# Full attention: scores from two-part float32r stacks with two heads side by side, in another order of issue

## The reference

```python
q = (x @ wq.T).reshape(b, s, NH, HD).transpose(0, 2, 1, 3)
k = (x @ wk_a.T @ wk_b.T).reshape(b, s, NH, HD).transpose(0, 2, 1, 3)
v = (x @ wv_a.T @ wv_b.T).reshape(b, s, NH, HD).transpose(0, 2, 1, 3)
q = _apply_decoupled_rope(q, cosf, sinf, DROPE)
k = _apply_decoupled_rope(k, cosf, sinf, DROPE)
scores = jnp.einsum('bhqd,bhkd->bhqk', q, k) / np.float32(np.sqrt(HD))
attn = jax.nn.softmax(scores, axis=-1)
out = jnp.einsum('bhqk,bhkd->bhqd', attn, v)
out = out.transpose(0, 2, 1, 3).reshape(b, s, NH * HD)
return out @ wo.T
```

## Time and profile before

| | us |
|---|---|
| median of 3 runs | 4984.07 (4980.47 to 4986.2) |
| the profiled execution | 4988.85 |
| its span, first to last instruction | 4987.1 |
| projections and setup, to the first row score | 315 |
| full attention, first column score to last copy of the sums | 364.6 to 1921.7 |

### The profile page before, as it was taken

One profiled execution on the slowest core, in us unless ns is written; L12 is line 12 of the kernel. 1 busy time (PEld: TensorE's weight loads), 2 busy tenths in 40 slices (PEclk: granted clock), 3 DMA queues, 4 the chain that ended last, 5 costly groups with the idle time before them and its releaser, 6 DMA issues. The chain is left out here.

```text
span 4987.1 us, 97545 instructions
## 1 busy us (share of the span) xinstructions
PE 4492.7 (90%) x27802; PEld 2756.6 (55%) x27802; DVE 3736.9 (75%) x8989; ACT 2758.3 (55%) x6177; POOL 1684.7 (34%) x2440
## 2 busy tenths in 40 slices
PE   4779999999999997489999996999799999997998
PEld 2423333332323333367777775888577777776887
DVE  6978888888888884878888885554488887884554
ACT  1317666766666774056666664333466666663333
POOL 3620000000000001445555554433355555554555
PEclk8869999999999998799999997999999999998999
DMA  4762323232323323610000001111100000002221
GB/s 156 244 137 40 56 43 59 40 59 40 59 40 59 46 35 124 205 43 26 25 23 26 24 25 50 43 53 46 48 25 24 26 24 25 23 23 81 78 64 50
DMA packets 385590, 288.63 MB, mean 58 GB/s; under 512 B 64284, under 2 KB 346392, under 8 KB 385056
## 3 DMA queue, kind: packets, MB, share of 16 engines
q1 hardware_dynamic: 385056, 282.19, 23.6%
HBM read 178.74 MB, written 102.83 MB: 56 GB/s over the span
## 5 line engine op out<-in xcount | busy, mean ns | idle before, releaser
L949 DVE TENSOR_REDUCE fa_mx<-fa_pR 128x1 f32<-128x512 f32 x2048 | 1276.3, 684 | 207.8 <-PE fa_pR L826 198.5
L925 ACT ACTIVATE fa_P<-fa_pS 128x512 f32<-128x512 f32 x2048 | 1077.2, 601 | 531.1 <-PE fa_pS L849 528.3
L1557 POOL TENSOR_TENSOR wa_pn<-wa_pr,wa_ri 128x512 f32<-128x512 f32 x512 | 700.6, 1369 | 616.3 <-DVE wa_ri L1613 602.9
L826 PE MATMUL fa_pR<-fa_K,fa_Q 96*128 96x512 bf16 x2048 | 804.1, 393 | 29.3 <-DMA fa_K<-parts_d 28.8
L849 PE MATMUL fa_pS<-fa_Q,fa_K 98*128 98x512 bf16 x2048 | 784.2, 386 | 26.8 <-issue 22.4
L1179 POOL TENSOR_TENSOR ao_xn<-ao_xn,ao_mod 128x1024 f32<-128x1024 f32 x16 | 37.6, 2347 | 1742.3 <-DVE ao_xn L1144 1742.3
L1493 ACT ACTIVATE wa_pr<-wa_sm,wa_mn 128x256 f32<-128x256 f32 x1024 | 510.5, 502 | 178.3 <-DVE wa_mn L1605 176.9
L862 PE MATMUL fa_pO<-fa_P,fa_V 128*32 128x512 f32 x4096 | 552.0, 611 | 5.9 <-ACT fa_OT L914 5.2
L849 PEld LDWEIGHTS fa_pS<-fa_Q,fa_K 98*128 98x128 bf16 x2048 | 199.2, 98 | 638.2 <-ACT fa_P L925 437.5
L1345 PE MATMUL wa_pQK<-wa_wqkv,wa_xT 128*128 128x512 f32 x1536 | 420.6, 410 | 5.8 <-DVE wa_qa L1650 5.8
L2051 ACT ACTIVATE ff_gl<-ff_pG,ff_b 128x512 f32<-128x512 f32 x192 | 132.1, 688 | 475.4 <-PE ff_pG L1992 475.4
(11 more groups left out here) (191 smaller groups left out, 7358.4 us busy)
## 6 DMA issues: line engine op xcount, KB each, us to landing
parts_d<-pj_parts SPq DMA_DIRECT2D x96, 256.0 KB, 2.8
fa_Q<-parts_d SPq DMA_DIRECT2D x192, 128.0 KB, 4.7
fa_K<-parts_d SPq DMA_DIRECT2D x192, 128.0 KB, 7.3
v_d<-pj_v SPq DMA_DIRECT2D x16, 1024.0 KB, 6.0
fa_V<-v_d SPq DMA_DIRECT2D x32, 512.0 KB, 9.9
pj_x<-in_L_attn_x SPq DMA_DIRECT2D x16, 512.0 KB, 6.7
att_d<-fa_att SPq DMA_DIRECT2D x32, 256.0 KB, 3.2
ao_att<-att_d SPq DMA_DIRECT2D x16, 512.0 KB, 4.7
```

The source lines that it names most:

```text
L826: nc.tensor.matmul(row_tile(), Qs[0:SROWS, s, h, q * P:(q + 1) * P], Ks[0:SROWS, s, h, half * 512:(half + 1) * 512], start=True, stop=True ...
L925: nc.scalar.activation(Pr[:, k % 2, h, half * 512:(half + 1) * 512], pS[:, (s * exped.per + u) % T, :], ACT.Exp).then_inc(exped.sem, 1)
L949: nc.vector.tensor_reduce(mx[:, j // 2, j % 2:j % 2 + 1], row_tile(), AX.X, ALU.max).then_inc(row_free, 1)
L1557: nc.gpsimd.tensor_tensor(pn[:, hp % 2], pr[:, hp % 2], inv, ALU.mult).then_inc(s["weighted"].sem, 1)
```

## The change

q and k are split into two float32r parts instead of three bfloat16 ones; ScalarE writes the first, one subtraction on VectorE the second. `second` and `third` are gone. The stacks become float32r with three blocks of 16 rows to a head, and two heads stand in one stack: one at partitions 0 to 47 (maxima and ones at 48 and 49), one at 64 to 111 (112 and 113). Each score matmul has 48 or 50 rows, and those of the two heads follow each other, into different banks. VectorE reduces both heads' row scores at once, from a slot of two banks; there are two such slots (ROW_T).

A group is now taken in two halves of the queries, 8 steps to each. A step has the column scores of heads 0 and 1, both row pairs of the next group, the column scores of heads 2 and 3, and the sums of the step before. Maxima, copies, transposes, divisions and stores go by halves. The negative maximum is transposed in float32 and split after it; it reaches the stack by 16 DMAs to a group. Row scores run one group ahead, no longer two steps more. The first loads wait for the rows of ones. The constant `identb` and its copy in the setup are gone.

```diff
-Q_PARTS = (0, 1, 2, 0, 1, 0)
-K_PARTS = (0, 0, 0, 1, 1, 2)
+Q_PARTS = (0, 0, 1)
+K_PARTS = (0, 1, 0)
...
-        parts_d = dram("parts_d", [2, 3, D, B, N], BF16)
+        parts_d = dram("parts_d", [2, 2, D, B, N])
...
-        parts = sb("pj_parts", [P, 2, 2, 3, KT, CH], BF16)
-        res = sb("pj_res", [P, 2, KT, CH])
+        parts = sb("pj_parts", [P, 2, 2, 2, KT, CH], F32R)
...
-                def rest(n, p, qk):
+                def low(n, p, qk):
                     dve.wait_ge(hi_ready.sem, hi_ready.upto(n, qk + 1))
-                    if again(n):
-                        dve.wait_ge(lows.sem, lows.upto(n - 1, qk + 1))
-                    nc.vector.tensor_tensor(res[:, qk], (pQ, pK)[qk][:], parts[:, p, qk, 0],
-                                            ALU.subtract).then_inc(split.sem, 1)
-                def second(n, p, qk):
-                    dve.wait_ge(split.sem, split.upto(n, 2 * qk + 1))
-                    if later(n) and qk == 0:
-                        dve.wait_ge(stored.sems[p], stored.upto(n - 2))
-                    nc.vector.tensor_copy(parts[:, p, qk, 1], res[:, qk]).then_inc(split.sem, 1)
+                    nc.vector.tensor_tensor(parts[:, p, qk, 1], (pQ, pK)[qk][:], parts[:, p, qk, 0].bitcast(F32),
+                                            ALU.subtract).then_inc(lows.sem, 1)
                 def body(n, r, following=True):
                     if following:
-                        stats_of(n + 2, (r + 2) % R, range(0, 4))
-                    rest(n, r % 2, 0)
+                        stats_of(n + 2, (r + 2) % R, range(0, 6))
+                    low(n, r % 2, 0)
...
-                def third(n, p, qk):
-                    pool.wait_ge(split.sem, split.upto(n, 2 * qk + 2))
-                    nc.gpsimd.tensor_tensor(parts[:, p, qk, 2], res[:, qk], parts[:, p, qk, 1],
-                                            ALU.subtract).then_inc(lows.sem, 1)
...
+        Qs = sb("fa_Q", [P, NB, PAIRS, N], F32R)
+        Ks = sb("fa_K", [P, NB, PAIRS, N], F32R)
...
+        pS = ctx.enter_context(nc.psum_tensor("fa_pS", [P, T, HALF], F32))
+        pR = ctx.enter_context(nc.psum_tensor("fa_pR", [P, ROW_T, 2, HALF], F32))
+        pO = ctx.enter_context(nc.psum_tensor("fa_pO", [P, HALF], F32))
...
+                            src = parts_d[qk, part].rearrange("(g a e d) b t -> e d g a b t", d=HD, e=2, a=PAIRS)
+                            for e in range(2):
+                                at = e * TOP + slot * HD
+                                one = src[e][:, bass.ds(g, 1), :, bass.ds(b, 1), :]
+                                sp.dma_start(stack[at:at + HD, s].bitcast(F32),
+                                             one.rearrange("d g a b t -> d (g a) (b t)")).then_inc(stack_in.sems[s], 16)
...
+                def max_rows(n, s, half):
+                    sp.wait_ge(row_free, max_use(n, half) + 1)
                     for part in range(2):
+                        for e in range(2):
+                            for a in range(PAIRS):
+                                at, col = e * TOP + SROWS + part, (e * PAIRS + a) * QB
+                                dst = Qs[at:at + 1, s, a, half * HALF:(half + 1) * HALF].bitcast(F32)
+                                src = nrow[col:col + QB, s, half, part, :].bitcast(F32)
+                                sp.dma_start(dst, src).then_inc(max_in[half].sems[s], 16)
...
+                sp.wait_ge(ones, NB)
                 load(0, 0)
                 load(1, 1)
+                max_rows(0, 0, 0)
                 def body(n, s):
+                    max_rows(n, s, 1)
+                    if not (isinstance(n, int) and n + 2 >= GROUPS):
+                        load(n + 2, (s + 2) % NB)
                     if not is_first(n):
+                        store(n - 1, 1)
                     if not is_last(n):
+                        max_rows(n + 1, (s + 1) % NB, 0)
+                    store(n, 0)
                 drive(sp, body)
+                store(GROUPS - 1, 1)
...
+                def row_slot():
+                    base, k = use
+                    if not (isinstance(base, int) and base + k < ROW_T):
+                        pe.wait_ge(row_free, base + k - ROW_T + 1)
+                    use[1] += 1
+                    first = base if isinstance(base, int) else 0
+                    return pR[:, (first + k) % ROW_T]
...
+                    q, a, kh = j // (2 * PAIRS), j // 2 % PAIRS, j % 2
...
+                    slot = row_slot()
+                    for e in range(2):
+                        at = e * TOP
+                        last = nc.tensor.matmul(slot[:, e, :], Qs[at:at + SROWS, s, a, q * P:(q + 1) * P],
+                                                Ks[at:at + SROWS, s, a, kh * HALF:(kh + 1) * HALF],
+                                                start=True, stop=True)
                     last.then_inc(row_full, 1)
...
+                def turn_max(n, half):
+                    pe.wait_ge(neg.sem, neg.upto(n, half + 1))
+                    slot = row_slot()
+                    nc.tensor.transpose(slot[0:MCOLS, 0, 0:P], nm[:, half, :], ident[:]).then_inc(row_full, 1)
+                def scores(n, s, k, a):
+                    half, kb = k // KB, k % KB
+                    u = k * GH + 2 * a
+                    if kb == 0 and a == 0:
+                        pe.wait_ge(max_in[half].sems[s], max_in[half].upto(n))
+                    if not (is_first(n) and u < 2):
+                        pe.wait_ge(exped.sem, n * exped.per + u - 1)
+                    for e in range(2):
+                        at = e * TOP
+                        nc.tensor.matmul(pS[:, (s * exped.per + u + e) % T, :],
+                                         Ks[at:at + SROWS + 2, s, a, kb * P:(kb + 1) * P],
+                                         Qs[at:at + SROWS + 2, s, a, half * HALF:(half + 1) * HALF],
+                                         start=True, stop=True).then_inc(scored.sem, 1)
+                def sums(n, s, k):
+                    half, kb = k // KB, k % KB
+                    pe.wait_ge(exped.sem, exped.upto(n, (k + 1) * GH))
+                    for h in range(GH):
+                        last = nc.tensor.matmul(pO[h * 32:(h + 1) * 32, :], V[:, s, kb, h, :], Pr[:, k % 2, h, :],
+                                                start=(kb == 0), stop=(kb == KB - 1))
+                    last.then_inc(summed.sem, 1)
+                def turn_sums(n, half):
+                    pe.wait_ge(o_out.sem, o_out.upto(n, half + 1))
+                    slot = row_slot()
+                    for t in range(QB):
+                        last = nc.tensor.transpose(slot[:, 0, t * P:(t + 1) * P], OT[:, half, t * P:(t + 1) * P],
+                                                   ident[:])
+                    last.then_inc(row_full, 1)
...
+                    for k in range(STEPS):
+                        scores(n, s, k, 0)
+                        if not is_last(n):
+                            row_scores(n + 1, (s + 1) % NB, 2 * k)
+                            row_scores(n + 1, (s + 1) % NB, 2 * k + 1)
+                        scores(n, s, k, 1)
+                        if k > 0:
+                            sums(n, s, k - 1)
+                        elif not is_first(n):
+                            sums(n - 1, (s - 1) % NB, STEPS - 1)
                         if k == 0:
+                            turn_max(n, 1)
+                        if k == 2 and not is_first(n):
+                            turn_sums(n - 1, 1)
+                        if k == KB and not is_last(n):
+                            turn_max(n + 1, 0)
+                        if k == KB + 2:
+                            turn_sums(n, 0)
...
+                def copy_out(n, half):
+                    act.wait_ge(summed.sem, summed.upto(n, (half + 1) * KB))
                     if not is_first(n):
+                        act.wait_ge(row_full, sums_use(n - 1, half) + 1)
+                    nc.scalar.copy(OT[:, half, :], pO[:]).then_inc(o_out.sem, 1)
                 def body(n, s):
+                    for k in range(STEPS):
                         for h in range(GH):
+                            u = k * GH + h
+                            act.wait_ge(scored.sem, scored.upto(n, u + 1))
+                            if h == 0 and not (is_first(n) and k < 2):
+                                act.wait_ge(summed.sem, n * STEPS + k - 1)
+                            nc.scalar.activation(Pr[:, k % 2, h, :], pS[:, (s * exped.per + u) % T, :],
+                                                 ACT.Exp).then_inc(exped.sem, 1)
                         if k == 0 and not is_first(n):
+                            copy_out(n - 1, 1)
+                        if k == KB:
+                            copy_out(n, 0)
...
+                    for e in range(2):
+                        last = nc.vector.memset(Ks[e * TOP + 32:e * TOP + 64, s].bitcast(F32), 1.0)
...
```

(23 more changed lines are left out.)

373 lines of the change are left out of this document (115 added, 258 removed).

## The result

| | before | after |
|---|---|---|
| median, us | 4984.0 (4980.5 to 4986.2, 4 runs) | 4840.6 (4837.1 to 4850.1, 4 runs) |
| span of the profiled execution | 4987.1 | 4835.1 |
| first row score, first column score | 315.1, 364.6 | 270.2, 307.3 |
| last copy of the sums | 1921.7 | 1773.1 |

The ratio is 0.9717, with an interval of 0.9702 to 0.9732: 2.8% faster. The forecast was 4780. Of the 152 us that the span lost, 57 lie ahead of the first column score (forecast 32), 91 between it and the last copy of the sums (forecast 172), and 3 behind. So two terms were off, in opposite directions.

What follows compares the result with a forecast made beforehand. It took TensorE's order of issue to bound the attention. From the span of 4987 us it took 172 for attention and 33 for projections, added 1 for the attention's start: 4783, median 3 lower, 4780; range 4700 to 4885.

Steps and rivals of the forecast that it cites:

- forecast case: Whole kernel: the main account, 4780 us, with its own range of 4735 to 4840 and a chance of 0.59.
- The signs: Trace readings named beforehand, mostly in the attention: intervals of sums, copies, stores, pairs, and engine idle times, to confirm or refute.
- The pair: Attention scores on TensorE: two heads' matmuls share the array, a pair taking 0.25 us, between 0.22 and 0.47.
- The chain: Attention step: column scores, exp, second column scores and sums wait in turn, 2.40 to 2.64 us, taken as 2.50.
- VectorE: Attention reduces: one of 1024 elements every 1.13 us, two a step; no group under 39.0 us.
- What stands between the steps: Attention, per group: transposes, maxima and copy of the sums cost 2.1 us, as before the change.
- The start of the attention: Before the first column score: loads wait for the ones, fewer reduces make up for it; cost 0 to 2, taken 1 us.
- The projections: Projection chunks: VectorE's stall goes, DMA is next at 11.5 us; gain 33 us, between 12 and 48.
- The maxima's DMAs: Attention: 16 small DMAs a group for 4, issued eight steps ahead; counted as nothing, 5 us once if late.
- Loads in line: Rival, attention: each float32r load keeps 0.19 us to itself, step 2.68, about 4873 us; chance 0.13.
- One after the other: Rival, attention: a pair's heads don't share the array, TensorE needs 2.97 us a step, about 5012 us; chance 0.10.
- Clock: Rival, attention: TensorE's clock falls to 1.2 GHz, a step takes near 4 us, the whole kernel 5500 us; chance 0.02.

Runs made afterwards that it cites:

- rows_apart: Changed kernel with each step's second row-score pair moved from before to after the second pair of column scores: 4971.0 us.
- high_halves: Changed kernel whose column scores alone read the high half of each float32 word as bfloat16, weights and columns: 4750.7 us.
- all_out: Changed kernel with the loop of its full attention written out, same instructions in the same order: 4756.8 us.
- swap_waits: Changed kernel with ScalarE's two waits before a step's first exp exchanged, old sums first and score last: 4825.4 us.
- best: Changed kernel with loop written out, each step's sums in two halves, and first loads waiting only for their own set's ones: 4711.3 us.
- before_two_subtractions: Kernel before without GpSimd's two subtractions for the third bfloat16 parts, the second part stored in their place: 4922.7 us.
- same_rows: Changed kernel with both heads of each pair reading rows 0 to 49, so their matmuls can't share the array: 5377 us.
- split_sums: Changed kernel with each step's sums taken in two halves of 256 queries, one behind each pair of column scores: 4814.0 us.

## Why the prediction held, and where it was wrong

Forecast 4780, measured 4840.6, inside the range of 4700 to 4885 and on the side that had 0.88. The forecast case's own range ended at 4840, so the time is at its edge, and two misses partly cancel in it: the attention fell 81 us short and the projections gave 25 more. With the first alone it would have been about 4861 (4780 and 81, an estimate). That the number is as near as it is, is in part luck.

*The signs.* Most came out on one side: sums every 2.69 us (2.40 to 2.65 named), copies 22.2 apart (20 to 22), ScalarE idle once for 0.41 a step (twice 0.2), and VectorE idle for 0.33, where over 0.3 was to mean a wrong account. It is the miss of the chain that they show. The first stores are 10.3 apart (11 to 12). The pairs, within 0.01 us, and the reduces came as named.

*The pair.* 0.25 us forecast. Two row pairs in a row last 0.66 from first start to last end and one record 0.40: 0.26 from pair to pair. The size is right. One reason for it isn't: I had the two loads of a pair one after the other in the array's time, 2 x 0.122, and their records start together, as those of the matmuls do. The two heads start within 0.01, inside the 0.12.

*The chain.* Right as a mechanism, as rows_apart showed: S0, exp, S1, sums. Its size was the term that failed: 2.40 to 2.64, took 2.50, measured 2.69. Two steps of the working were wrong. I added the float32r load "once at S0 and once at S1, partly the same time" and took the middle; both count in full, 0.19 together, as high_halves showed with bfloat16 in their place. And I read the chain from the last group, which stands behind the loop, while the steps it was to stand for run inside. The loop adds 0.08 at the first exp, as all_out and swap_waits showed: an instruction of ScalarE's sequencer between the score and the exp. Behind the loop and in bfloat16 the 0.43 of the earlier trace rows is back, so that the two causes make up the whole 0.18 of S0 to the exp. 2.40 + 0.19 + 0.08 = 2.67 against 2.69. There was no term for this, because in the kernel before, whose bound was TensorE's issue, it cost nothing. By the groups: 31 times 44.4 in place of 42.1 are 71 us, and the turns 47 in place of 40: together the 78 to 81 that the stage fell short.

*VectorE.* 1.13 for each reduce: two take 2.36, the last record being 1.23, so 1.13 from start to start. Right, and not the bound: 0.33 idle in a step. In all_out and best it is nearer, with 1160.65 busy of 1180 us in the latter, 98%; whether it is the bound there was not tried:

```profile
420.00:1600.00 1180.00, 1173.18 (x11060) 448.62 (x11060) 1160.65 (x1181) 996.62 (x1852) 0.00 (x0) 1.00 0.36 56
```

*What stands between the steps.* 2.1 a group forecast, 1.4 measured.

*The start of the attention.* The first row score lost 12 us to the wait for the ones (258.2 without, 270.2 with it), 13 forecast; the prologue took 37.0 against 49.5, 38 forecast. Cost 0 to 2: right.

*The projections.* 33 forecast, bounds 12 and 48, and before_two_subtractions gained 57 at the first row score. The reason (GpSimd's third parts stall VectorE) was right. What failed is the price of what comes next: I scaled DMA's share with the bytes, 11.5 us, but DMA carried them at 374 GB/s, in longer rows, and the chunk came to 10.3 (15 times 1.2 are 18 us). I named DMA as the next bound and had no term for TensorE, which is busy 95% of this stretch; which of the two sets the 10.3 isn't shown. And the first chunk, whose stores left at 85.9 and now at 78.2, has the same stall, which I had counted for 15 chunks alone.

*The maxima's DMAs.* No wait of the column scores from 420 to 1700 us ends with a DMA. Nothing, as forecast.

*The rivals.* "Loads in line" had the step at 2.68 and the time at 4873: a number near the measured one by a reason that is false, as each load doesn't keep its time to itself; only the two that nothing covers do. "One after the other" was tried as same_rows: 3.06 in place of 2.97, and 5377 in place of 5012, as it was priced without the clock. "Clock", at 0.02, did not come as a low level throughout. But behind each turn of the loop the clock is low for 3 to 14 us in the changed kernel, and turns followed by 54 and 38 us of it kept split_sums from its gain.

## What to carry to other kernels

Once engines wait for each other in a ring, every tenth of a microsecond on it counts in full, those too that a full engine used to hide: an uncovered weight load of a wide type, an instruction of the sequencer between an arrival and the work, and so the order of two waits. Read the links of such a ring where the code runs that they stand for, in the loop and not behind it. And price the turns of a loop together with the clock that falls after them: a version that is tighter in its steps can lose there what it gains.
